# Dense experts on Trainium2: a one-column gelu ahead of each pass's first wait, and the last products handed over by row block

## What is computed

```python
def _L1_ffn_ref(hidden_states, gate_w, w1, b1, w2, b2):
    x = hidden_states.reshape(-1, 512)                  # 2048 rows
    router_logits = x @ gate_w.T
    _, sel = top_k(router_logits.sum(axis=0), 2)        # the same 2 experts for all rows
    rw = softmax(router_logits[:, sel], axis=1)
    h = gelu(einsum('nd,kdf->knf', x, w1[sel]) + b1[sel][:, None, :])   # 2048 hidden columns
    y = einsum('knf,kfd->knd', h, w2[sel]) + b2[sel][:, None, :]
    return einsum('nk,knd->nd', rw, y)
x = x + _L1_ffn_ref(layernorm(x), ...)                  # the output
```

## Time and profile before

| | us |
|---|---|
| median of 3 runs | 1602.61 (1598.06 to 1603.4) |
| the profiled execution's own time | 1595.51 |
| its span | 1593.8 |
| PE busy | 1393.5 (87%) |
| DVE busy | 937.2 (59%) |
| POOL busy | 780.1 (49%) |
| ACT busy | 709.2 (44%) |
| mean granted TensorE clock | 0.923 |

### The profile page before, as it was taken

The page is one execution under the profiler, slowest core; times in us unless marked ns, Lnnn a source line. Parts: engine busy times, 40 slices in busy tenths (PEclk is TensorE's granted clock), DMA queues, the critical chain, the costliest instruction groups (busy, mean ns, idle before and its releaser), DMA issues.

```text
span 1593.8 us, 18874 instructions
## 1 busy us (share of the span) xinstructions
PE 1393.5 (87%) x6080; PEld 1031.7 (65%) x6080; DVE 937.2 (59%) x1186; ACT 709.2 (44%) x1303; POOL 780.1 (49%) x607
## 2 busy tenths in 40 slices
PE   6988982699899988986276999999999999999998
PEld 3534442566566656664166787878787887878786
DVE  2768767989999999997773224241414224241413
ACT  4445433366666766664143333333333333333332
POOL 0000000888888888884631545444544545444442
PEclk9899895699999999999555999999999999999999
DMA  3202225477887987863656900010000100010000
GB/s 104 108 28 79 107 78 195 140 242 246 295 289 231 312 280 264 268 199 104 212 198 212 356 14 0 0 66 1 14 0 15 51 13 0 0 53 0 0 0 26
DMA packets 78202, 191.29 MB, mean 120 GB/s; under 512 B 10856, under 2 KB 15752, under 8 KB 77120
## 3 DMA queue, kind: packets, MB, share of 16 engines
q1 hardware_dynamic: 64832, 157.03, 29.1%
q0 software_dynamic: 6400, 20.98, 4.2%
q10 hardware_dynamic: 6912, 12.59, 2.1%
HBM read 152.55 MB, written 38.01 MB: 120 GB/s over the span
## 4 chain that ended last, share of the span: by engine, by line
PE 58%; DVE 21%; issue 10%; ACT 4%; DMA 3%; POOL 3%; ACTq 0%; SPq 0%; DVEq 0%; POOLq 0%
PE decay L1668 22%; PE bank L1657 21%; DVE decay L1243 10%; DVE S L1252 3%; PE bank L1467 2%; PE decay L1423 2%; PE bank L1554 1%; PE bank L1430 1%; PE bank L1527 1%; DVE XH L1110 1%; POOL S L723 1%; DMA XG<-xn_rows,gcol 1%; PE bank L1487 1%; PE decay L1477 1%; PE decay L1473 1%
## 5 line engine op out<-in xcount | busy, mean ns | idle before, releaser
L1380 DVE CAST HFH<-HF 128x512 fp32r<-128x512 f32 x128 | 59.0, 461 | 497.0 <-ACT HF L1041 497.0
L811 POOL TENSOR_TENSOR W2L<-W2R,W2H 128x512 fp32r<-128x512 f32 x128 | 172.3, 1346 | 347.9 <-ACT W2H L1036 347.9
L723 POOL TENSOR_TENSOR S<-DTU,Bb 128x1024 f32<-128x1024 f32 x128 | 301.6, 2385 | 26.1 <-DVE row_hot L1225 21.7
L1243 DVE TENSOR_TENSOR_SCAN decay<-decay,S 128x1024 f32<-128x1024 f32 x128 | 292.9, 2288 | 0.0
L1657 PE MATMUL bank<-XSH,W1H 128*128 128x512 f32 x512 | 202.9, 396 | 4.2 <-POOL W1L L807 4.2
L1668 PE MATMUL decay<-W2H,HFH 128*128 128x512 f32 x512 | 200.6, 392 | 5.3 <-DVE HFL L1382 5.3
L1657 PE MATMUL bank<-XSH,W1L 128*128 128x512 f32 x512 | 202.9, 396 | 0.0
L1657 PE MATMUL bank<-XSL,W1H 128*128 128x512 f32 x512 | 202.2, 395 | 0.0
L1668 PE MATMUL decay<-W2L,HFH 128*128 128x512 f32 x512 | 200.0, 391 | 0.0
L1668 PE MATMUL decay<-W2H,HFL 128*128 128x512 f32 x512 | 199.8, 390 | 0.0
L807 POOL TENSOR_TENSOR W1L<-W1R,W1H 128x512 fp32r<-128x512 f32 x128 | 171.0, 1336 | 48.0 <-ACT W1H L1027 48.0
(11 more groups left out here) (212 smaller groups left out, 2105.7 us busy)
## 6 DMA issues: line engine op xcount, KB each, us to landing
WGU<-in_L_ffn_gate_w SPq DMA_DIRECT2D x48, 384.0 KB
WGU<-in_L_ffn_up_w SPq DMA_DIRECT2D x48, 384.0 KB
WD<-in_L_ffn_down_w SPq DMA_DIRECT2D x48, 384.0 KB
Bb<-bc_rows SPq DMA_DIRECT2D x32, 512.0 KB, 7.2
Cb<-bc_rows SPq DMA_DIRECT2D x32, 512.0 KB, 9.2
expert_rows<-YT ACTq DMA_DIRECT2D x48, 256.0 KB
W1R<-in_L_ffn_w SPq DMA_DIRECT2D x6, 1024.0 KB, 13.7
W2R<-in_L_ffn_w SPq DMA_DIRECT2D x6, 1024.0 KB, 14.1
```

The lines of the kernel that those rows point to most:

```text
L723: pool.tensor_tensor(S[u % NP][:], DTU[:, ds(b, 1), c, :].to_broadcast([P, PAIR, L]), Bb[j][:], ALU.mult).then_inc(dbu_ready, 1)
L811: pool.tensor_tensor(W2L[f % 2][:], W2R[:, ds(e, 1), f, :].rearrange("p e d -> p (e d)"), W2H[f % 2][:].bitcast(F32), ALU.subtract).then_i ...
L1243: dve.tensor_tensor_scan(flat, flat, S[u % NP][:].rearrange("p i l -> p (i l)"), 0.0, ALU.mult, ALU.add).then_inc(scan_done, 1)
```

## The change

ACT gets one more gelu in each pass: one column of zeros (`zero`, which exists already) into a new tile `gelu_first` of 128x1. It stands after split_w1(1) and before the wait of gelu(0), has no wait, and nothing reads its output.

PE signals a new semaphore `rows_done` after the third matmul of row blocks 0, 1 and 2 of down(15); for the last row block `down2_done` stays. DVE waits for these ahead of each of the four additions of L1397, where it had one wait for all. Each of the four now signals `y2_added`, and the counts waited for are changed to match (PE, DVE, SP).

SP stores O in four DMAs of 256 KB, each after its row block's addition, and counts four stores for each `tb`.

```diff
+        gelu_first = sb(h, "gelu_first", [P, 1])
...
+        rows_done = sem("rows_done")
...
                 if tb:
-                    sp.wait_ge(out_stored, tb * DMA)
+                    sp.wait_ge(out_stored, tb * T * DMA)
...
-                sp.wait_ge(y2_added, (tb + 1) * TOP + 1)
-                sp.dma_start(out[tb].rearrange("(t p) d -> p t d", p=P), O[:]).then_inc(out_stored, DMA)
-            sp.wait_ge(out_stored, B * DMA)
+                for t in range(T):
+                    sp.wait_ge(y2_added, (tb * TOP + TOP - 1) * T + t + 2)
+                    sp.dma_start(out[tb, t * P:(t + 1) * P, :], O[:, t, :]).then_inc(out_stored, DMA)
+            sp.wait_ge(out_stored, B * T * DMA)
...
                         if f + 1 < FT:
                             split_w1(f + 1)
+                        if f == 0:
+                            act.activation(gelu_first[:], zero[:, 0:1], ACT.Gelu_apprx_tanh)
                         gelu(f)
...
-                    dve.wait_ge(down2_done, it + (FT + 2))
                     for t in range(T):
                         w = rwf[:, ds(e, 1), tb * T + t:tb * T + t + 1].rearrange("p e t -> p (e t)")
                         dve.wait_ge(ob_ready, e * T + (tb * (TOP * T) + t + 1))
-                        ins = dve.scalar_tensor_tensor(O[:, t, :], PS[t][:], w, O[:, t, :], ALU.mult, ALU.add)
-                    ins.then_inc(y2_added, 1)
-                    dve.wait_ge(y2_added, e + (tb * TOP + 2))
+                        if t < T - 1:
+                            dve.wait_ge(rows_done, e * (T - 1) + (tb * (TOP * (T - 1)) + t + 1))
+                        else:
+                            dve.wait_ge(down2_done, it + (FT + 2))
+                        dve.scalar_tensor_tensor(O[:, t, :], PS[t][:], w, O[:, t, :], ALU.mult, ALU.add
+                                                 ).then_inc(y2_added, 1)
+                    dve.wait_ge(y2_added, e * T + (tb * (TOP * T) + T + 1))
...
                         if f == 0:
-                            pe.wait_ge(y2_added, tb * TOP + e + 1)
+                            pe.wait_ge(y2_added, tb * (TOP * T) + e * T + 1)
...
+                            if f == FT - 1 and t < T - 1:
+                                ins.then_inc(rows_done, 1)
                         ins.then_inc(down2_done, 1)
```

## The result

| | before | after |
|---|---|---|
| median of 7 runs, us | 1599.64 (1596.27 to 1603.4) | 1609.2 (1606.15 to 1615.31) |
| ratio to before | | 1.0068, 95% interval 1.0051 to 1.0084 |
| profiled execution, us | 1595.51 | 1609.2 |
| span | 1593.8 | 1607.5 |
| first matmul of the dense part, start | 869.55 | 873.96 |

The change makes the kernel slower by 0.7%. Of the 13.7 us between the two spans, 4.4 lie ahead of the dense part, in code that the change doesn't touch; over all the profiles of this study that start varied from 866.8 to 879.9, and it is not shown what moves it.

A forecast was written before the change was run, and what follows sets the result against it. The prediction took PE's matmuls to set the time in the dense part; +10.3 - 0.9 - 2.95 = +6.4 on 1602.6 gave 1609.0 us. Likeliest case's range 1606 to 1612, with others 1596 to 1613.

The forecast's parts named there:

- The load moves and is hidden: On ACT at a pass boundary, the 1.28 us table load moves ahead of gelu(0)'s wait, at no cost; gelu(0) runs 1.30 earlier.
- POOL first, HFH and HFL behind it: At a boundary POOL's W2L(1) starts at +1.37, HFH at +1.39 to +1.54; taking turns puts down(0)'s first matmul at +4.78.
- 1.47 at all seven boundaries, +10.3: down(0)'s first matmul starts 1.47 us later at each boundary but the first pass's, +10.3 us in all.
- rival 2: HFH goes first at the three boundaries with a new `tb`: +3.1 us in all, 1605.7 us; chance 0.16.
- The first pass, -0.9: With no additions before it, HFH and HFL start ahead of POOL and PE's wait goes whole: -0.9 us.
- Edit 2 inside the run, 0: The signals by row block move nothing before the end: 0, at most 0.1 us per pass each way.
- The end, -2.95: After PE's last matmul, earlier bank additions and four stores together shorten the kernel's end by 2.95 us.
- Rivals 1, 3 and 4: No turns at the boundary: 1594.8 us, 0.17; load stays under gelu(0): 1599.7, 0.07; end gains only 1.0: 1611.0, 0.10.

The follow-up runs named there:

- e4: The changed kernel with POOL, at f = 0, waiting for HFL after W1L(1), then making W1L(2), W2L(1), W2L(2): 1591.77 us, ratio 0.9965.
- e9: e6 with the bias additions behind HFL of f = 9 to 12 in place of 4 to 7: 1588.52 us, ratio 0.9932.
- e2: The changed kernel without the gelu of one column and its tile: 1596.75 us, ratio 0.9992.
- e1: The kernel before with only the gelu of one column and its tile added: 1609.0 us, ratio 1.0088.
- e3: The changed kernel with gelu_first placed behind all other tiles: 1607.76 us, ratio 1.0076.
- e5: The changed kernel with the four bias additions moved from the pass's end to behind HFL of f = 4 to 7: 1605.84 us, ratio 1.0046.
- e6: e5 with gelu_first placed behind all other tiles: 1602.9 us, ratio 1.0024.
- e8: e6 without the gelu of one column and its tile: 1610.58 us, ratio 1.0065.
- e7: e4 with gelu_first placed behind all other tiles: 1591.94 us, ratio 0.9954.

## Why the prediction was right, and where it was not

It said 1609.0 us and slower; 1609.2 was measured. That closeness is luck: two errors of 3 us cancel. The shift that I forecast was +6.4; measured is +9.6 between the medians, and by the interval of the ratio 8.2 to 13.4 us. The median of before that I started from, 1602.6, came out 3.0 us lower with more runs. The direction and the mechanism were right; the size of the loss was forecast too small.

*The load moves and is hidden:* right. It stands 4.4 us before s, and gelu(0) starts without it; the new gelu took 0.20, within its bounds.

*POOL first, HFH and HFL behind it:* right, in place and size. Forecast: POOL +1.37, HFH from +1.39 to +1.54, matmul +4.78. Measured +1.37, +1.41 and +4.81 at the head of the second pass; over the seven boundaries HFH started at +1.37 to +1.72. e4 shows the cause, since POOL's order alone takes the long casts away, and e9 shows it from the other side. The Trainium skill (SBUF — State Buffer, section "SBUF: two separate sides") words it more sharply than the section that the prediction draws on: between GpSimd's operations and VectorE's that use both ports or have two SBUF inputs there is an exclusive lock, held for a whole instruction by whichever starts first. The rows at 968.80 and 1061.47 agree: with POOL 0.04 ahead HFH took 1.54, and level with it 0.43, so 0.04 us decide over 1.1 us. They don't agree to the hundredth, as a held HFH ends 0.29 after POOL and not its own 0.43.

*1.47 at all seven boundaries, +10.3:* too much. It was so at five (between matmuls 2.57 against 1.06, +7.6); at two HFH was level with POOL, won, and the loss was 0.38 (+0.8), where the prediction's bound for this case was 0.35. That is rival 2 at two of its three places, and +8.3 together.

*The first pass, -0.9:* right, no wait for HFL there.

*Edit 2 inside the run, 0:* within its bound; e2 has 0.06 per boundary.

*The end, -2.95:* right, -3.17.

*The step that failed is what I left out of the sum:* I priced a longer wait at its own length. Two waits of 2.2 us were each followed by a fall of the granted clock, with matmuls at 0.43 in place of 0.23 apart: the 30 matmuls behind such a wait took 1.55 longer than behind one without a fall, +3.1 for two. And the tile of 4 bytes per partition was not even named, so it stood at nothing: it moved the addresses of the tiles behind it and made each of 128 steps 0.013 longer, +1.7. Forecast for stretch and end: 10.3 - 0.9 - 2.95 = +6.4. Measured: 8.3 - 0.9 + 3.1 + 1.7 - 3.2 = +9.0, where the trace has 12.46 - 3.17 = +9.3; 0.2 of what is left is the one slow matmul more at the start of the stretch. The time between the medians was +9.6.

*Rivals 1, 3 and 4* didn't come true: turns were taken, the load moved, and the end gained in full.

## What to carry to other kernels

Before you make an operation earlier, list what else its engine's neighbours will then start earlier, and who shares something with them. Here a hidden load pulled POOL's subtraction ahead as well, from 0.19 behind HFL to 0.04 ahead of HFH. Free the engine that has to go first (in e9 it is DVE, with its bias additions moved), and then the same edit pays. When you move a piece of work forward, look at the first pass, where its input may come last.

## What the runs showed of the hardware

- The clock of PE fell after short waits. In the changed kernel, e1 and e3 together there were 14 waits for HFL of 2.1 to 2.2 us, and behind 7 of them a fall to 1.2 GHz of 3.4 us each; behind 7 waits of 1.0 us there were none. In e5, e6 and e8 it fell during a standstill of 13 to 14 us. What sets apart the waits with and without a fall was not tried.
- Where the tiles lie matters a little to the matmuls: `gelu_first` in front of six names (b1n, b1T, b2b, XS and the two fp32r operands XSH and XSL) made the step of 24 matmuls 5.540 in place of 5.527. The change is in the spacing of the matmuls (from the last of an up product to the first of a down product 0.239 in place of 0.230 in the changed kernel), and went with the tile's place in every pair tried (changed and e3, e4 and e7, e5 and e6). Which of the six does it was not tried.
- DVE took 0.37 to 0.73 us from the end of a pass's last addition to the next cast, where HF was there already (changed kernel, e1, e3, e4, e7). It differs from one place in the program to the next, by 0.35 between two boundaries of the same kind, and why was not tried; where two engines are 0.04 apart, this decided.
